# Two row blocks together at the start of a chain of products, on one core

## The reference

```
def layer(x, cond, ffn):              # once with the L0 weights, once with the L1 weights
    return x + ffn(cond(x))

L0 cond:  w_eff = quantize((weight + B @ A * 0.5) / scale) * scale + B @ A * 0.5
          # quantize: nearest of 64 codebook levels, found by thresholds, scale per 128 columns
          x @ w_eff.T
L0 ffn:   x @ W_base.T + b + (top-2 of 8 experts, softmax weights) low-rank terms of rank 16
L1 cond:  x @ weight.T + bias + scale[adapter of the sequence] * (x @ a.T) @ b.T
L1 ffn:   x @ base_W + (top-2 of 8 experts) low-rank terms of rank 16
```

## Time and profile before

| | |
|---|---|
| median of three runs | 882.62 us (882.16 to 883.49) |
| profiled execution, its own time | 883.0 us |
| span of the profile | 880.8 us |
| TensorE busy | 876.4 us, 4514 matmuls |
| VectorE busy | 768.7 us |
| ScalarE busy | 326.6 us |
| rows 0 to 8 of the first product on TensorE | 5.40 to 130.30 us |

### The profile page before, as it was taken

How to read it: one execution, slowest core, us unless ns; L and a number is a source line. 1 busy time by engine, 2 the same in 40 slices (tenths; PEclk the granted TensorE clock), 3 DMA queues, 4 the chain that set the end, 5 groups by cost and what they waited for, 6 DMA issues and landing times.

```text
span 880.8 us, 13800 instructions
## 1 busy us (share of the span) xinstructions
PE 876.4 (100%) x4514; PEld 768.5 (87%) x4514; DVE 768.7 (87%) x1844; ACT 326.6 (37%) x525; POOL 156.1 (18%) x310
## 2 busy tenths in 40 slices
PE   9999999999999999999999999999999999999998
PEld 8999998888998888888888888888888888888887
DVE  6999999687687868778889999999999999999995
ACT  6588788421434424231322322222223223222221
POOL 0210020111002001412212212212212312312310
PEclk9999999999999999999999999999999999999999
DMA  9533340675412042484777977987887987887975
GB/s 346 210 103 120 126 138 24 210 265 182 145 49 94 2 144 74 143 321 167 256 272 254 320 262 272 313 289 256 305 298 256 303 286 270 304 288 259 313 256 218
DMA packets 62610, 191.93 MB, mean 218 GB/s; under 512 B 8256, under 2 KB 12742, under 8 KB 60620
## 3 DMA queue, kind: packets, MB, share of 16 engines
q1 hardware_dynamic: 50282, 158.92, 51.3%
q0 software_dynamic: 11968, 31.88, 12.5%
q10 hardware_dynamic: 290, 0.26, 0.1%
HBM read 158.80 MB, written 32.76 MB: 217 GB/s over the span
## 4 chain that ended last, share of the span: by engine, by line
PE 98%; DMA 1%; SPq 0%; DVE 0%; ACT 0%; issue 0%; DVEq 0%
PE bank L950 17%; PE bank L600 15%; PE bank L602 15%; PE bank L601 15%; PE bank L974 9%; PE bank L932 7%; PE bank L918 5%; PE bank L978 4%; PE bank L927 2%; PE bank L1075 2%; PE bank L756 2%; PE bank L644 1%; PE bank L651 1%; DMA m_raw<-m1t 1%; PE bank L882 0%; PE bank L880 0%
## 5 line engine op out<-in xcount | busy, mean ns | idle before, releaser
L950 PE MATMUL bank<-g_hi,xs 128*128 128x512 f32 x440 | 140.1, 390 | 0.0
L563 POOL DMA_DIRECT2D p1sel<-p_scratch x128 | 65.6, 512 | 263.1 <-issue 263.1
L2046 DVE STREAM_TRANSPOSE bank<-ranks_raw 32x64 f32<-32x64 f32 x416 | 106.5, 256 | 6.2
L950 PEld LDWEIGHTS bank<-g_hi,xs 128*128 128x128 f32 x440 | 82.6, 188 | 17.1
L974 PE MATMUL bank<-t_hi,xs 128*128 128x512 f32 x336 | 91.1, 392 | 0.0
L950 PE MATMUL bank<-g_lo,xs 128*128 128x512 f32 x220 | 86.5, 393 | 0.0
L600 PE MATMUL bank<-gx,xs 128*128 128x304 f32 x256 | 77.6, 303 | 0.0
L602 PE MATMUL bank<-gx,xs 128*128 128x304 f32 x256 | 77.4, 303 | 0.0
L601 PE MATMUL bank<-gx,xs 128*128 128x304 f32 x256 | 77.1, 301 | 0.0
L1525 DVE TENSOR_TENSOR xs<-x_raw,xs 128x1024 fp32r<-128x1024 f32 x60 | 74.2, 1259 | 1.9 <-ACT xs L1152 1.0
L974 PEld LDWEIGHTS bank<-t_hi,xs 128*128 128x128 f32 x336 | 63.1, 188 | 14.2
(11 more groups left out here) (397 smaller groups left out, 2114.0 us busy)
## 6 DMA issues: line engine op xcount, KB each, us to landing
t_hi<-t_scratch SPq DMA_DIRECT2D x82, 512.0 KB, 5.8
t_lo<-t_scratch SPq DMA_DIRECT2D x82, 512.0 KB, 6.7
x_raw<-xq SPq DMA_DIRECT2D x16, 1024.0 KB, 7.0
out<-ost SPq DMA_DIRECT2D x63, 256.0 KB, 6.8
p1sel<-p_scratch POOLq DMA_DIRECT2D x64, 192.0 KB, 6.0
w_raw<-wall SPq DMA_DIRECT2D x15, 512.0 KB, 4.6
w<-e_scratch SPq DMA_DIRECT2D x6, 1024.0 KB, 5.1
ea<-e_scratch POOLq DMA_DIRECT2D x8, 644.0 KB, 5.6
```

The costliest lines, as they stand in the source:

```text
L563: pool.dma_start(f(p1sel[b][64 * s:64 * s + STK, cs]), p1_dram[bass.ds(i * STK, STK), cs]).then_inc(sems[b], 16)
L950: mm = nc.tensor.matmul(bk[j][:], l[:, c, :], m[:, c, :], start=first and c + k == 0, stop=c + k == KH + 1, skip_group_check=True)
L2046: ins = nc.vector.transpose(turned[ks, :, ts], ranked[ts, :, ks])
```

## The change

Row 1 is now computed with row 0 from the first chunk on: six groups with each chunk for chunks 0 to 4. For chunks 5, 6 and 7 the work goes row by row: row 0 takes its three groups through the three chunks, and then row 1 does. Row 1's second and third group need two more banks, and get banks 2 and 3 (`EXTRA`), which `delta` and the codebook steps used. So the codebook steps move to bank 0, and the second half of `delta(0)`, which writes banks 2 and 3, waits until all three groups of row 1 have been copied out (`e_ev` 6). `delta(0)` moves from inside row 1 into row 2, after its second chunk. The codebook steps move to the last three chunks of row 1. The copy of row 1's third group moves, on ScalarE, from after step 6 of round 0 to before the round.

```diff
-DELTA0 = (1, 2, 4)
+EXTRA = {(1, 1): 2, (1, 2): 3}
+DELTA0 = (2, 0, 1)
-CB_AT = {(1, 5): 0, (1, 7): 1, (2, 2): 2}
+CB_AT = {(5, 0): 0, (6, 0): 1, (7, 1): 2}
+N_PAIR = 5
-EV_AT = {(0, 7): [(1, 0), (1, 1)], (0, 6): [(1, 2)], (0, 4): [(2, 0), (2, 1)],
+EV_AT = {(0, 7): [(1, 0), (1, 1), (1, 2)], (0, 4): [(2, 0), (2, 1)],
-        group = lambda n, g: bk[RING + (3 * n + g) % RING]
+        group = lambda n, g: bk[EXTRA[n, g]] if (n, g) in EXTRA else bk[RING + (3 * n + g) % RING]
...
                     if t:
                         pe.wait_ge(wd_ok[u], t)
                         pe.wait_ge(d_cp[u], t)
+                    elif u:
+                        pe.wait_ge(e_ev, 6)
...
-            ALL = ((0, 0), (0, 1), (0, 2), (1, 0))
+            ROW = [tuple((r, g) for g in range(3)) for r in range(2)]
...
-            pair_high(0, ALL[3:4])
-            pair_low(0, ALL[3:4])
+            pair_high(0, ROW[1])
+            pair_low(0, ROW[1])
             pe.wait_ge(m1_hi_s, M1_HI[1])
-            pair_high(1, ALL[1:4])
-            pair_low(1)
-            for c in range(2, KC - 1):
+            pair_high(1, ROW[0][1:3] + ROW[1])
+            pair_low(1, ROW[0] + ROW[1])
+            for c in range(2, N_PAIR):
...
-            pe.wait_ge(m1_hi_s, M1_HI[KC - 1])
-            for part in (ALL[0:1], ALL[1:3], ALL[3:4]):
-                pair_high(KC - 1, part)
-                pair_low(KC - 1, part)
-            for r in range(1, KC + 1):
+            for row in ROW:
+                for c in range(N_PAIR, KC):
+                    pe.wait_ge(m1_hi_s, M1_HI[c])
+                    for n, g in row:
+                        pair_high(c, ((n, g),))
+                        pair_low(c, ((n, g),))
+                        if n and (c, g) in CB_AT:
+                            codebook_step(CB_AT[c, g])
+            for r in range(2, KC + 1):
```

More of the change, by code:

```diff
@@ L619, in codebook_step @@
                     pe.wait_ge(cols_ok, 1)
-                    nc.tensor.matmul(bk[3][0:LV, 0:1], tt_[0:1, 0:LV], one1[0:1, 0:1], start=True, stop=True)
-                    nc.tensor.matmul(bk[3][0:LV, 1:2], cb[0:1, :], one1[0:1, 0:1], start=True, stop=True)
-                    nc.tensor.matmul(bk[3][0:LV, 2:3], reach[0:1, :], one1[0:1, 0:1], start=True, stop=True).then_inc(cols_mm, 1)
+                    nc.tensor.matmul(bk[0][0:LV, 0:1], tt_[0:1, 0:LV], one1[0:1, 0:1], start=True, stop=True)
+                    nc.tensor.matmul(bk[0][0:LV, 1:2], cb[0:1, :], one1[0:1, 0:1], start=True, stop=True)
+                    nc.tensor.matmul(bk[0][0:LV, 2:3], reach[0:1, :], one1[0:1, 0:1], start=True, stop=True).then_inc(cols_mm, 1)
                 if k == 1:
                     pe.wait_ge(cols_ok, 2)
-                    nc.tensor.matmul(bk[3][0:LV, 3:4], tri, cols[:, 2:3], start=True, stop=True).then_inc(cols_mm, 1)
+                    nc.tensor.matmul(bk[0][0:LV, 3:4], tri, cols[:, 2:3], start=True, stop=True).then_inc(cols_mm, 1)
                 if k == 2:
                     pe.wait_ge(cols_ok, 3)
-                    nc.tensor.matmul(bk[3][:, 64:256], ones[0:LV, 0:1].to_broadcast([LV, P]),
+                    nc.tensor.matmul(bk[0][:, 64:256], ones[0:LV, 0:1].to_broadcast([LV, P]),
                                      selm[:].rearrange("p a b -> p (a b)"), start=True, stop=True).then_inc(cols_mm, 1)
@@ L645, in pair_high, with pair_low @@
                                              stop=False, skip_group_check=True)
-            def pair_low(c, groups=ALL):
-                pe.wait_ge(m1_lo_s, c + 2 if c or groups[0][1] else 1)
+            def pair_low(c, groups):
+                pe.wait_ge(m1_lo_s, 1 if c == 0 and groups == ROW[0][0:1] else c + 2)
                 for row, g in groups:
@@ L656, in _ @@
             pe.wait_ge(m1_hi_s, 1)
-            pair_high(0, ALL[0:1])
-            pair_low(0, ALL[0:1])
+            pair_high(0, ROW[0][0:1])
+            pair_low(0, ROW[0][0:1])
             pe.wait_ge(m1_hi_s, M1_HI[0])
-            pair_high(0, ALL[1:3])
+            pair_high(0, ROW[0][1:3])
             pe.wait_ge(m1_hi_s, M1_HI[1] - 1)
-            pair_high(1, ALL[0:1])
-            pair_low(0, ALL[1:3])
-            pair_high(0, ALL[3:4])
-            pair_low(0, ALL[3:4])
+            pair_high(1, ROW[0][0:1])
+            pair_low(0, ROW[0][1:3])
+            pair_high(0, ROW[1])
+            pair_low(0, ROW[1])
             pe.wait_ge(m1_hi_s, M1_HI[1])
-            pair_high(1, ALL[1:4])
-            pair_low(1)
-            for c in range(2, KC - 1):
+            pair_high(1, ROW[0][1:3] + ROW[1])
+            pair_low(1, ROW[0] + ROW[1])
+            for c in range(2, N_PAIR):
                 if c in ld_part:
                     pe.wait_ge(m1_hi_s, M1_HI[c] - 1)
-                    pair_high(c, (ALL[0], ALL[3]))
+                    pair_high(c, (ROW[0][0], ROW[1][0]))
                     pe.wait_ge(m1_hi_s, M1_HI[c])
-                    pair_high(c, ALL[1:3])
+                    pair_high(c, ROW[0][1:3] + ROW[1][1:3])
                 else:
                     pe.wait_ge(m1_hi_s, M1_HI[c])
-                    pair_high(c, ALL)
-                pair_low(c)
-            pe.wait_ge(m1_hi_s, M1_HI[KC - 1])
-            for part in (ALL[0:1], ALL[1:3], ALL[3:4]):
-                pair_high(KC - 1, part)
-                pair_low(KC - 1, part)
-            for r in range(1, KC + 1):
+                    pair_high(c, ROW[0] + ROW[1])
+                pair_low(c, ROW[0] + ROW[1])
+            for row in ROW:
[7 more added lines that the diff above has]
+            for r in range(2, KC + 1):
                 pe.wait_ge(ws_hi, r + 3)
@@ L686, in _ @@
                 for g, (n0, n) in enumerate(A_COLS):
-                    if 3 * r + g < RING:
-                        continue
                     pe.wait_ge(e_ev, 3 * r + g - RING + 1)
@@ L692, in _ @@
                                            m1_hi[:, c, n0:n0 + n], m1_lo[:, c, n0:n0 + n], c == 0, c == KC - 1)
-                        if r == 1 and (g, c) in CB_AT:
-                            codebook_step(CB_AT[g, c])
                         if (r, g, c) == DELTA0:
@@ L1615, in _ @@
             v.wait_ge(cols_mm, 1)
-            link(nc.vector.tensor_copy(cols[:, 0:3], bk[3][0:LV, 0:3]))
+            link(nc.vector.tensor_copy(cols[:, 0:3], bk[0][0:LV, 0:3]))
             nc.vector.tensor_scalar(cols[:, 0:2], cols[:, 0:2], cols[:, 2:3], None, ALU.mult).then_inc(cols_ok, 1)
@@ L1620, in _ @@
             v.wait_ge(cols_mm, 2)
-            link(nc.vector.tensor_copy(cols[:, 3:4], bk[3][0:LV, 3:4]))
+            link(nc.vector.tensor_copy(cols[:, 3:4], bk[0][0:LV, 3:4]))
             for i in range(3):
@@ L1626, in _ @@
             v.wait_ge(cols_mm, 3)
-            nc.vector.tensor_copy(thr[:], bk[3][:, 64:128])
-            nc.vector.tensor_copy(vcomp[:], bk[3][:, 128:192])
-            nc.vector.tensor_copy(valid[:], bk[3][:, 192:256]).then_inc(comp_ok, 1)
+            nc.vector.tensor_copy(thr[:], bk[0][:, 64:128])
+            nc.vector.tensor_copy(vcomp[:], bk[0][:, 128:192])
+            nc.vector.tensor_copy(valid[:], bk[0][:, 192:256]).then_inc(comp_ok, 1)
             v.wait_ge(comp_ok, 1)
```

## The result

| | before | after |
|---|---|---|
| median of 12 runs of each, side by side | 882.76 us (882.16 to 885.16) | 884.3 us (883.74 to 886.42) |
| ratio | | 1.0018, 95% interval 1.0011 to 1.0026 |
| profiled execution, its own time | 883.0 us | 885.49 us |
| span of the profile | 880.8 us | 883.8 us |

The change makes the kernel slower by 1.5 us (interval 1.0 to 2.3). Predicted were 884.1 us, so +1.5. The profiled execution of the changed kernel is later than its median by 1.2 us. The reason is in its first microseconds, and it must be taken off before any of its times is compared with the forecast.

A forecast was written before the change was run, and what follows sets the result against it. Only TensorE's idle time was taken to move the time: -0.80 us gained in the arrival, +2.32 of waits at rows 3 and 5, sum +1.52, so 884.1 us from a median of 882.62; range 882.0 to 885.6.

The forecast's parts named there:

- arrival: While the M1 chunks arrive, TensorE's remaining 0.80 us of waiting after 8.07 us is all gained; bounds 0 and 0.80.
- `delta(0)`: The first delta on TensorE moves from 32.51 to 34.36 us: 2.65 later by order, 0.80 earlier by arrival, +1.85.
- new wait for the copies: Second half of `delta(0)` at 35.29 needs `e_ev` 6, expected at about 34.0: no wait, 1.3 us to spare.
- VectorE's first L1651: VectorE's first use of the delta result, before at 33.85, comes 1.85 us later, at about 35.7; bounds +1.4 and +2.65.
- row 3: In the first product, low weights ready at 50.74, TensorE there at 49.68: it waits, row 3 at +0.41 against before.
- row 5: In the first product, low weights ready at 79.07 set the start at 79.22 against 77.70: +1.52 us.
- row 6: In the first product, weights ready at 90.65, TensorE there at 91.91: no wait.
- TensorE less late than VectorE by: After row 6 TensorE is 1.52 and VectorE 1.85 us later than before, 0.33 apart, with no later wait found.
- The early gain stays: Rival, 12%: VectorE and ScalarE win back some 2 us before row 5, TensorE keeps its 0.80: 881.8, up to 883.
- The copy of row 1 holds `delta(0)`: Rival, 10%: `e_ev` 6 comes after 35.29 and delays TensorE and VectorE; 885.3 with a store 2.5 us later.
- The change doesn't fill the wait: Rival, 6%: arrival gains 0 because another piece of each chunk is late; row 5 at +2.32, total 884.9.
- The clock: By the Trainium skill's rule, TensorE's new waits could lower its clock and cost more than their length; no chance given.

The follow-up runs named there:

- The version finished group by group: Changed kernel with row 1's last three chunks taken group by group and the first `delta` inside its last group: 882.78 us, ratio 1.0002 to the kernel before.
- the version with the earlier splits: Changed kernel with the splits of the weights of rows 3, 5 and 6 each one step earlier: 882.03 us, measured again 882.46 us, ratio 0.9994 both times.

## Why the prediction was right

| step | predicted | measured |
|---|---|---|
| arrival | 0.80 us won | 0.83 up to row 3; no gap after the row at 9.53 |
| `delta(0)` | 34.36 | 34.35 with chunk 1 in time; 35.77, less 1.46, is 34.31 |
| new wait for the copies | none, 1.3 us to spare | none, 1.3 us |
| VectorE's first L1651 | +1.85 | +1.63 with chunk 1 in time |
| row 3 | waits about 1.1, isn't added | waits 0.94 by the starts (0.77 in brackets); without that wait row 5 waits 0.62 longer |
| row 5 | decides, waits about 1.1, 0.15 for the restart | decides; waits 1.01 by the starts (0.85 in brackets); 0.10 + 0.08 |
| row 6 | no wait | none |
| TensorE less late than VectorE by | 0.33 | 0.30 |
| end | +1.5 | +1.5 (1.0 to 2.3); +1.3 again |

The one step that failed is the sentence that nothing of VectorE's own takes up the shift. 0.22 us of it was taken up. Before, VectorE's first L1651 is put down to TensorE's L613 with an idle time of 0.28. But it also had its own small steps behind the thresholds: from `thr` at 31.71 to L1651 at 33.85 are 2.14 us. From the start of `delta(0)` it was 1.34 us, and in every kernel with a later `delta` it is 1.13 (34.35 to 35.48, 35.77 to 36.90, 35.22 to 36.35). So TensorE's result was there at 32.51 + 1.13 = 33.64, and what came last before was VectorE's own chain. The version finished group by group bears this out: its `delta(0)` is earlier than before, the wait names no releaser, and from `thr` to this instruction are again 2.16 us (31.53 to 33.69). The shift is counted from that: 1.85 - 0.21 = 1.64, and 1.63 was measured. The forecast for an execution with chunk 1 in time should have been +1.3. From the row of 8.07 (9.53 in the changed kernel) to the product after row 8 the traces have 1.27 us more. The mechanism held, step by step; that the median came out at the forecast's +1.5 to the tenth is partly luck, and no proof of the 0.2.

The rivals. *The early gain stays* would need `w_lo` of row 5 unshifted: it is shifted by as much as the first L1651. *The copy of row 1 holds `delta(0)`*: no gap at 36.70. *The change doesn't fill the wait*: it does, 0.83 us less in front of row 3, and 0.90 us at the product after row 8 between the traces of the late `delta` alone and of the whole change. *The clock*: the windows of the changed kernel (a stretch from and to, its length, busy time of each engine, granted clock, DMA) that hold the two waits:

```profile
50.48:77.70 27.22, 26.45 (x149) 25.97 (x148) 25.56 (x26) 22.32 (x35) 3.98 (x6) 1.00 0.42 126
77.70:130.30 52.60, 51.75 (x289) 50.76 (x288) 48.91 (x46) 44.98 (x67) 8.23 (x13) 1.00 0.39 121
```

The granted clock is 1.00, the upper level, in both, and TensorE is idle for 0.77 and 0.85 us, no more than the waits themselves. The section of the Trainium skill that the prediction names ("TensorE: Matmul & The Clock Gate", "HAM oscillation — how this bites in real kernels") is about a kernel in which each burst of matmuls is shorter than the wait behind it. Nothing of the kind stands here: two waits of about 1 us, 28 us apart, in a stretch that is otherwise full. This case is not that one, and no run here tests the section's rule.

What stays open: whether the version with the earlier splits is faster than before. Its two measurements, -0.84 and -0.40 us, lie on the same side, but differ from each other by as much as identical kernels do. What VectorE does in the 0.28 us before its first L1651 isn't shown either; the program has a register load (`value_load`) there, which the profile doesn't count. Why the first columns of chunk 1 come at different times wasn't tried.

## What to carry over

- Beside the list of waits, read the distances: the end of what is needed against the start of what needs it. The list of before had one wait of 0.4 us after the first product; the price of this change was at a place that had none, with 0.48 us to spare.
- Work that moves from the middle to the start pushes back what stands between, and here that was the one result which the other two engines waited for. Before a gain of 0.8 us is taken from the start, the fixed slots that hang on this result need at least as much distance as the engines drift apart, 2.4 us here (0.8 + 1.6). One number in a table, row 5's slot, gave most of the loss back.
- Where an engine's idle time has a releaser, look for the second latest of what it waited for: it takes up part of the shift.

## What the runs showed of the hardware

- ScalarE could start on the first columns of a chunk that is loaded at the start at 6.69 us in one execution, and at 7.92 and 8.13 in others of nearly the same program. With the new order 1.42 us of it were still there at `delta(0)`. A change of 1 us can't be read from one profile of each kernel, unless the arrival is taken off.
- TensorE started its first matmul 0.10 us after VectorE's result was ready (80.25 and 80.35), and lost 0.08 more before the second.
- From the first of the 512-column matmuls of `delta(0)` to VectorE's first use of its banks went 1.13 us, in three kernels with different starts. In the program VectorE waits for the fourth of these matmuls, which starts 0.69 us after the first (32.51 and 33.20 before): so it starts about 0.4 us after the start of the one that it waits for.
